# Norm means asked for earlier, Newton rounds in two units, a convolution wait by bank

## The reference, cut to what matters

```
x = x + window_attention(group_norm(x))   # 7x7 windows, shifted by 3, 8 heads, qkv and output projection
x = x + conv3x3(group_norm(x), w)         # w: mean |w| per filter times sign(w)
```

## Time and profile before

| | |
|---|---|
| median of 3 runs | 3406.44 us |
| the profiled execution's own time | 3410.27 us |
| its span, first to last instruction | 3408.5 us |
| busy: PE, DVE, ACT, POOL | 93%, 85%, 72%, 67% |
| busy: PE's weight loads (PEld, beside PE) | 78% |
| mean granted TensorE clock | 0.995 of full speed |

### The profile page before, as it was taken

How to read it: one execution, slowest core, us unless ns; L and a number is a source line. 1 busy time by engine, 2 the same in 40 slices (tenths; PEclk the granted TensorE clock), 3 DMA queues, 4 the chain that set the end, 5 groups by cost and what they waited for, 6 DMA issues and landing times.

```text
span 3408.5 us, 153595 instructions
## 1 busy us (share of the span) xinstructions
PE 3169.9 (93%) x64139; PEld 2662.6 (78%) x64139; DVE 2908.6 (85%) x6143; ACT 2453.5 (72%) x5473; POOL 2298.3 (67%) x3235
## 2 busy tenths in 40 slices
PE   2899999999999999999999999999999999999997
PEld 1678888878888878888878888878888778888785
DVE  5688888888888888888888888888888888888885
ACT  1777777777777777777777777777777777777772
POOL 4476667766667766667766667766667766667763
PEclk9999999999999999999999999999999999999998
DMA  2112112222112222112222112222112222112111
GB/s 61 37 45 54 47 45 51 52 52 54 47 44 51 52 52 54 47 44 51 52 52 54 47 43 53 52 52 54 47 43 52 53 52 53 47 42 52 35 36 36
DMA packets 352640, 165.96 MB, mean 49 GB/s; under 512 B 148048, under 2 KB 351952, under 8 KB 351952
## 3 DMA queue, kind: packets, MB, share of 16 engines
q1 hardware_dynamic: 351952, 156.13, 18.8%
HBM read 53.31 MB, written 51.38 MB: 31 GB/s over the span
## 4 chain that ended last, share of the span: by engine, by line
PE 59%; DVE 17%; POOL 11%; issue 9%; ACT 2%; SPq 1%; DMA 1%; DVEq 0%; POOLq 0%; ACTq 0%
PE conv_ps L994 16%; PE qkv_ps L876 11%; PE scores_ps L889 8%; PE probsT_ps L900 7%; PE attn_ps L913 5%; PE misc_ps L965 4%; DVE s_sb L747 4%; PE attn_ps L917 4%; DVE plane_lo L759 3%; POOL s_sb L432 3%; POOL gn_y L420 3%; PE misc_ps L956 2%; POOL gn_t L419 2%; DVE s_max L752 2%; PE misc_ps L962 2%
## 5 line engine op out<-in xcount | busy, mean ns | idle before, releaser
L432 POOL TENSOR_TENSOR s_sb<-s_sb,s_max 113x392 f32<-113x392 f32 x1024 | 962.7, 940 | 962.1 <-DVE s_max L752 961.4
L494 ACT COPY probsT<-probsT_ps 128x392 f32<-128x392 f32 x1024 | 495.9, 484 | 323.7 <-PE probsT_ps L900 307.1
L487 ACT ACTIVATE probs<-s_sb 113x392 f32<-113x392 f32 x1024 | 552.7, 540 | 159.7 <-POOL s_sb L432 157.2
L459 POOL TENSOR_TENSOR plane<-x_n 128x224 f32<-128x224 f32 x896 | 641.6, 737 | 18.7
L900 PE MATMUL probsT_ps<-ident,probs 113*128 113x113 f32 x4096 | 584.7, 265 | 50.0 <-ACT probsT L494 49.9
L752 DVE TENSOR_REDUCE s_max<-s_sb 113x8 f32<-113x392 f32 x1024 | 574.6, 561 | 35.3
L747 DVE TENSOR_TENSOR s_sb<-scores_ps,bias 113x392 f32<-113x392 f32 x1024 | 565.9, 553 | 19.3 <-PE scores_ps L889 11.4
L555 ACT COPY v<-qkv_ps 64x256 f32<-64x256 f32 (+2 forms) x1280 | 390.8, 324 | 207.1 <-PE qkv_ps L876 201.1
L900 PEld LDWEIGHTS probsT_ps<-ident,probs 113*128 113x128 f32 x4096 | 431.4, 141 | 104.8 <-ACT probs L487 63.8
L994 PE MATMUL conv_ps<-plane_hi,wc_hi 128*128 128x224 f16 x2688 | 482.3, 262 | 23.2 <-DVE conv_y L821 19.8
L994 PE MATMUL conv_ps<-plane_hi,wc_lo 128*128 128x224 f16 x2688 | 477.7, 260 | 0.0
(11 more groups left out here) (135 smaller groups left out, 6307.4 us busy)
## 6 DMA issues: line engine op xcount, KB each, us to landing
x_in<-in_x_dram SPq DMA_DIRECT2D x224, 224.0 KB, 3.1
recip_wide<-recip SPq DMA_DIRECT2D x1024, 49.0 KB
out_dram<-x_out SPq DMA_DIRECT2D x224, 224.0 KB, 2.3
x<-in_L_conv_w_dram SPq DMA_DIRECT2D x1, 576.0 KB
x<-L_conv_pruning_mask_dram SPq DMA_DIRECT2D x1, 576.0 KB
x_n<-_conv_rel_pos_table_dram SPq DMA_DIRECT2D x14, 10.7 KB
x_n<-in_mask_dram SPq DMA_DIRECT2D x1, 196.0 KB
plane<-n_L_conv_qkv_weight_dram SPq DMA_DIRECT2D x1, 192.0 KB
```

Of the source, the lines that this page charges most:

```text
L432: nc.gpsimd.tensor_tensor(s, s, top, ALU.subtract).then_inc(sub_ready, 1)
L459: last = nc.gpsimd.tensor_tensor(plane[:, t % 2, j], *sums[j])
L487: nc.scalar.activation(probs[0:QP, slot % 2, :, :, 0:N], s_sb[0:QP, slot % 4], ACT.Exp)\
L494: nc.scalar.copy(probsT[:, g % PT_SLOTS], probsT_ps[:].rearrange("p (w n) -> p w n", n=ODD)[:, :, 0:N])\
```

## The change

Three edits. The places of three of the four norm jobs move up: gn2's first from (6, END) to (6, MID), gn1's from (21, MID) and (22, END) to (20, MID) and (21, MID). With the sorting of the jobs, VectorE's parts of them move along: its gn1 mean copy from unit 21 to unit 20, its gn1 seed from unit 22 to unit 21. GpSimd's rounds of gn1 are divided: two in unit 22, behind the plane sums, the third and the shift in unit 23, behind sub(23). gn2's stay in unit 8. And a convolution tile's first matmul waits only until the tile before has read planes 0 and 1, its nineteenth until that one has read all.

```diff
-G2_JOBS = ((6, END), (7, MID))
+G2_JOBS = ((6, MID), (7, MID))
-G1_JOBS = ((21, MID), (22, END))
+G1_JOBS = ((20, MID), (21, MID))
+FIRST_ROUNDS = 2
...
-            def newton(gn, img):
+            def newton(gn, img, rounds):
-                done = [0]
+                done = [2 * rounds.start]
...
-                for _ in range(NEWTON):
+                for _ in rounds:
...
-                ts(gn.shift[:], ...).then_inc(gn.ready, 1)
+                if rounds.stop == NEWTON:
+                    ts(gn.shift[:], ...).then_inc(gn.ready, 1)
...
-                    for gn, jobs, shift in ((gn1, G1_JOBS, 1), (gn2, G2_JOBS, -1)):
-                        if u == jobs[1][0] + 1 and live(i, shift):
-                            newton(gn, i + shift)
+                    if u == G2_JOBS[1][0] + 1 and live(i, -1):
+                        newton(gn2, i - 1, range(NEWTON))
+                    if u == G1_JOBS[1][0] + 2 and live(i, 1):
+                        newton(gn1, i + 1, range(FIRST_ROUNDS, NEWTON))
...                     # behind the plane sums of the unit:
+                    if u == G1_JOBS[1][0] + 1 and live(i, 1):
+                        newton(gn1, i + 1, range(FIRST_ROUNDS))
...                     # conv, on TensorE:
-                    if n == 0:
+                    if n == 0 and img * TILES + k > 0:
+                        pe.wait_ge(conv_sums, (img * TILES + k - 1) * 4 + 1)
+                    if n == 2 * 3 * KW:
                         need(pe, conv_sums, (img * TILES + k) * 4)
```

More of the change, by code:

```diff
@@ L417, in newton @@
                 pool.wait_ge(gn.ready_steps, (img + 1) * 3)
-                for _ in range(NEWTON):
+                for _ in rounds:
                     then(ts(gn.t[:], gn.y[:], gn.y[:], gn.half[:], ALU.mult, ALU.mult))
                     then(ts(gn.y[:], gn.t[:], three_halves[:], gn.y[:], ALU.add, ALU.mult))
-                ts(gn.shift[:], gn.kept_out[:], gn.mean[:], gn.y[:], ALU.subtract, ALU.mult).then_inc(gn.ready, 1)
+                if rounds.stop == NEWTON:
+                    ts(gn.shift[:], gn.kept_out[:], gn.mean[:], gn.y[:], ALU.subtract, ALU.mult).then_inc(gn.ready, 1)
             pool.wait_ge(setup_done, 1)
```

## The result

The changed kernel takes 3506.68 us (median of 4 runs, 3503.79 to 3510.10), the kernel before 3406.89 us. The ratio is 1.029, 95% interval 1.0277 to 1.0303. The forecast was slower, 3443 us; the loss is 100 us and not 37. One of experiment 11's six runs took 10370 us at a mean granted clock of 0.44 and is left out of its time.

What follows compares the result with a forecast made beforehand. TensorE, busy 93% of the span, was taken as the bound, with at most 4.66 us an image to gain. 1.50 us late less 0.26 gained, times 30 images, added 37.2 to 3406.44 us: 3443 us, range 3402 to 3462.

Steps and rivals of the forecast that it cites:

- Step 3: By VectorE's list, proj waits for the seed's copy behind gn1's second job and starts 1.50 us later than before.
- step 2: By TensorE's own list, proj behind the late tout starts 1.26 us later than before.
- The rounds' term: Dividing gn1's Newton rounds on POOL gains the 0.26 us of idle time before sub(23) in each image.
- The sum: A delayed image costs 1.50 - 0.26 = 1.24 us; over 30 images 37.2 us, giving 3443 us.
- Takes away 0.28 us an image, and nothing comes of it: The convolution's wait by bank removes a 0.28 us wait in unit 20, which runs into tout's wait: no gain.
- gn2's term: Moving gn2's first job to (6, MID) gives 0; the 0.4 us wait for gn_var stays.
- A: Rival: the 1.66 us standstill in front of values of unit 25 absorbs the loss, 3406 us; chance 0.12.
- B: Rival: jobs asked for ahead answer in time, waits go and nothing follows, about 3370 us; chance 0.10.
- C: Rival: POOL's chain to x_n loses its stretches, 1.6 us, plus 0.26, about 3385 us; chance 0.05.

Runs made afterwards that it cites:

- experiment 11: Kernel before with gn1's jobs moved, VectorE's copies first, gn1's rounds in unit 21, gn2's in unit 7, tok_hi of row 0 behind probsT: 3481.34 us.
- experiment 8: Kernel before with gn1's two jobs moved and VectorE's parts of them put first in units 20 and 21: 3409.73 us, ratio 1.0003.
- experiment 3: Kernel before with gn1's Newton rounds divided over units 22 and 23 and nothing else: 3404.43 us, ratio 0.9995.
- experiment 2: Kernel before with gn1's two jobs moved to (20, MID) and (21, MID), all rounds still in unit 23: 3471.08 us, ratio 1.0188.
- 4: Changed kernel with 28 small unread matmuls in front of tout in unit 20: 3473.39 us, ratio 1.0195.
- experiment 7: Kernel of experiment 2 with 48 small unread matmuls in front of tout in unit 20: 3457.94 us, ratio 1.0149.
- Experiments 1: Changed kernel with gn1's jobs and rounds put back, gn2's move and the wait by bank kept: 3415.40 us, ratio 1.0025.
- 5: Kernel before with the convolution's wait divided by bank and nothing else: 3415.19 us, ratio 1.0020.
- experiment 6: Kernel before with a second, always fulfilled wait before each convolution tile's nineteenth matmul, the first wait left whole: 3416.69 us, ratio 1.0023.

## Why the prediction was wrong in its size

**The direction and its mechanism held.** tout waits for the mean copy (1.91 us, expected about 2), because VectorE takes it behind `plane_lo` of unit 20; experiment 8 shows it, since the loss goes when only the copies move.

**Step 3 was short by 0.23 us.** From gn2's bias (L692 before), a mark in each image, proj starts at 1567.09 - 1518.24 = 48.85 us before and at 867.34 - 816.76 = 50.58 us after: 1.73 us late and not 1.50. Mean, deviation and variance took 865.52 - 863.56 = 1.96 us and not 1.50; `s_sb`, `s_max` and `plane_lo` behind them took 1.60 and not 1.81. The deviation took 0.61 us and ends with the sub beside it, the pair of variance took 1.20 and each ends with one of POOL's two plane sums:

```profile
863.19 1.15 POOL L434 TENSOR_TENSOR s_sb<-s_sb,s_max 113x392 f32<-113x392 f32 x1 [1.10 <-DVE s_max L757]
864.31 1.27 POOL L462 TENSOR_TENSOR plane<-x_n 128x224 f32<-128x224 f32 x2
```

In experiment 8 POOL stands idle beside the pair, and it took 0.35 us:

```profile
1150.72 0.35 DVE L703 SCALAR_TENSOR_TENSOR gn_var<-gn_dev,gn_mv 128x1 f32<-128x1 f32 x2
```

By the Trainium skill's rule that the prediction weighed (page "SBUF — State Buffer", section "Who interferes with whom") they would be held here, and the prediction put that at 0.2 us an image; the trace agrees with it. On TensorE's side step 2 left out the 0.65 us wait for `gn_var`. With it TensorE's own list reaches proj as late as the seed's copy does, and proj shows no wait.

**The rounds' term was right in number by luck.** POOL's chain lost 0.34 us in the changed kernel (8.89 against 9.23) where 0.26 was forecast for dividing the rounds. But it is 9.21 with the rounds divided and nothing moved (experiment 3), and 8.73 with the jobs moved and the rounds whole (experiment 2). So the moved jobs made the chain shorter: VectorE's part left unit 22, and sub(23) came without idle time and took 0.84 us and not 1.15. The division gave 0.02 us alone, and the changed kernel, which has it beside gn2's move and the wait by bank, is 0.16 longer than experiment 2. That sub(23) becomes late and reaches TensorE as a wait in turn_probs was foreseen; its size was not, 1.15 us, and the wait in front of values was gone instead of holding. The sum of the two terms came out near: the image is late by what x_n is late, 1.73 - 0.34 = 1.39 us by the two chains, 103.63 - 102.27 = 1.36 by the stretches. The forecast was 1.24.

**The step that failed is "The sum".** It multiplied 1.24 us by 30 images and took the granted clock to stay at 1.00, as in the earlier trace rows. The clock does not stay there. With experiment 2's prices 11 x 1.51 + 10 x 3.04 = 47 us of the 91 that the 29 images lost come from it; 29 x 1.38 = 40 come from the wait; 4 are left for the issue time. These are estimates: the prices are another kernel's, and TensorE's idle time put down to issue in front of scores is 9.3 us here, against 1.7 before. Its upper bound held one more hold of `gn_var` and nothing for the clock. That the standstill is what brings the clock down is shown by filling it (4 and 7), not by argument. The trace of before held the warning. A standstill of about 2 us was forecast, longer than those of its 29 images (1.66, once 1.74), and in its first image, where the pipeline still fills, it has one of 2.21 us, with the clock at 0.50 behind it:

```profile
152.69 0.93 PE L913 MATMUL attn_ps<-probsT,v 128*32 128x49 f32 x64 [2.21 <-ACT probsT L494]
```
```profile
154.00:160.78 6.78, 6.70 (x87) 5.41 (x79) 4.68 (x8) 3.86 (x10) 4.80 (x8) 0.50 0.17 33
```

A price was there too: the next image has 6.8 us at 0.50, from 191.5 on behind a standstill of 1.43 us, and takes 103.77 us. The page "TensorE: Matmul & The Clock Gate" of the Trainium skill, section "HAM oscillation — how this bites in real kernels", tells that idle gaps on TensorE bring its clock back to 1.2 GHz; the trace shows it at 0.50 behind this one. The gaps that the section tells of are longer than this one, so its example alone would not have priced it; here the measurement decides.

**"Takes away 0.28 us an image, and nothing comes of it" failed too.** Experiments 1 and 5 put the wait by bank at 6 to 9 us of loss, and experiment 6 shows that the added wait instructions bring as much without any effect of theirs. And the 0.28 us did not vanish: they made tout's standstill longer, 1.91 us against 1.61 in experiment 2, and there the clock fell in 16 images and not in 21, with 3 of the long stretches and not 10. The changed kernel is 35 us slower than experiment 2. By the prices above the clock makes some 18 of them (47 against 29) and the full-clock image, 0.14 us longer, some 4; how they divide between the three further edits was not measured edit by edit.

**gn2's term held**: its 0.4 us wait is there in every kernel that moved it and in every one that did not.

**Rivals.** A (the stall in front of values absorbs the delay) fell: the chain began late. B fell: VectorE answered late. C had its shorter chain, by 0.34 of the 1.9 us that it wanted, and not through the division.

## What to carry to other kernels

Asking earlier moves the wait from the asker to whoever is queued behind the answer. Where two engines hand on one buffer, look first at where the answering engine's copy stands in its own list, and move that with the request. A new standstill on TensorE in a nearly full stretch had a second price here, the granted clock behind it: look for a standstill of that length anywhere in the trace of before, and price it with a row at the lower level. And a term that comes out in number is still to be tested alone: the rounds' 0.26 us was another edit's gain. The best version here removed standstills by the order in the lists of the engines that TensorE waited for.

## What the runs showed of the hardware

A wait that is always fulfilled, 223 of them on TensorE, cost about 8 us, in some images only, with 8.5 us of idle time put down to issue in front of scores against 1.7. Added matmuls without a wait brought such idle time too (9.7 us against 0.2 in experiment 7).

Two VectorE instructions of one element a partition took 1.20 us beside GpSimd's plane sums and 0.35 us with GpSimd idle.

The clock fell behind standstills of about 1.1 us (4 of 29 images, and a fifth with 1.6), 1.61 (16), 1.91 (21) and 2.4 to 2.9 (all 29, in some already before its end), but behind 1.98 us in front of values in only 12, and behind 1.66 us there in none. The single standstill's length alone doesn't order them; what does was not settled.

So most of 100 us in 3400 came from about 1.9 us of standstill at one place in an image, and about half of that, by the prices above, from the clock behind it.
